# Work handed across three stage borders in a fused perceiver kernel: the wide stage's start, the cell's first weights, the context stage's turned contexts

## The reference

```
x = x + masked_attention(layernorm(x), ctx_1024, ctx_1024, mask)   # 16 heads of 16; 64 batches, 64 tokens each, 256 keys each
x = x + wide_attention(layernorm(x), context)     # 8 heads of 128; 4096 queries against 1024 keys of 192 features
#   sim = q k^T / sqrt(128); sim = (sim - mean) * 1.5 + mean; softmax; times v; times Wout; + bout
x = x + cell(layernorm(x))          # 6 nodes; q, k, v = ew * (earlier node @ We + be), attention of 8 heads,
#   node = act_w * attention + q; the projections We @ Wq (Wk, Wv) of a node can be multiplied ahead: 18 pairs
x = x + context_attention(layernorm(x), ctx_1024) # softmax(x ctx^T) ctx, 64 batches of 64 tokens against 256 keys
x = x + scan(layernorm(x)); x = x + ffn(layernorm(x))              # untouched
```

## Time and profile before

| | us |
|---|---|
| median of 3 executions | 3042.66 (3039.46 to 3043.7) |
| the profiled execution, own time | 3044.71 |
| its span in the trace | 3043.0 |
| mean granted TensorE clock | 0.978 |
| DVE, ACT, POOL busy | 2179.4 (72%), 2042.5 (67%), 1176.4 (39%) |

### The profile page before, as it was taken

How to read it: one execution, slowest core, us unless ns; L and a number is a source line. 1 busy time by engine, 2 the same in 40 slices (tenths; PEclk the granted TensorE clock), 3 DMA queues, 4 the chain that set the end, 5 groups by cost and what they waited for, 6 DMA issues and landing times. The chain is left out here.

```text
span 3043.0 us, 84864 instructions
## 1 busy us (share of the span) xinstructions
PE 2862.5 (94%) x32198; PEld 2233.0 (73%) x32198; DVE 2179.4 (72%) x5344; ACT 2042.5 (67%) x4144; POOL 1176.4 (39%) x962
## 2 busy tenths in 40 slices
PE   8999999799999999999979999999999998789899
PEld 6888888466666666666667887887888887566798
DVE  7888888676777767767636778777778776668543
ACT  6888888686777777777706776676667676333444
POOL 6777777476565555565601010011010000111210
PEclk9999999999999999999989999999999999899899
DMA  4111111187899898898961012111111110651000
GB/s 148 55 54 60 49 60 36 27 133 136 146 165 150 145 152 149 147 161 146 199 224 52 37 44 71 37 44 54 37 44 50 51 37 26 212 169 50 8 22 28
DMA packets 620990, 275.14 MB, mean 90 GB/s; under 512 B 548971, under 2 KB 593958, under 8 KB 620470
## 3 DMA queue, kind: packets, MB, share of 16 engines
...
## 5 line engine op out<-in xcount | busy, mean ns | idle before, releaser
L1335 POOL TENSOR_TENSOR front_parts<-wide_prob,front_parts 128x1024 f16<-128x1024 f32 x256 | 546.2, 2134 | 354.4 <-ACT front_parts L1556 280.1
L1544 ACT ACTIVATE wide_prob<-wide_score,wide_neg_max,wide_s_up 128x1024 f32<-128x1024 f32 x256 | 307.5, 1201 | 147.8 <-DVE wide_neg_max L1657 140.6
L1654 DVE TENSOR_REDUCE wide_row_max<-wide_score 128x1 f32<-128x1024 f32 x256 | 312.6, 1221 | 131.0 <-PE wide_score L1376 130.7
L1376 PE MATMUL wide_score<-wide_kT,wide_qT 128*128 128x512 f16 x1536 | 377.2, 382 | 6.2 <-ACT wide_prob L1544 4.7
L2012 POOL TENSOR_TENSOR cell_w<-cell_w_stage,cell_w 128x1536 fp32r<-128x1536 f32 x23 | 80.4, 3494 | 642.9 <-ACT cell_w L2280 642.9
L637 POOL TENSOR_TENSOR mask_prob<-mask_prob,mask_inv_sum 128x512 f32<-128x512 f32 x256 | 272.2, 1064 | 107.7 <-DVE mask_inv_sum L1020 105.3
L885 ACT ACTIVATE mask_prob<-mask_prob,mask_row_min 128x256 f32<-128x256 f32 x512 | 255.0, 502 | 47.7 <-DVE mask_row_min L968 47.4
L1556 ACT ACTIVATE front_parts<-wide_prob 128x1024 f16<-128x1024 f32 x256 | 269.8, 1054 | 17.6 <-ACT wide_prob L1544 8.1
L1376 PEld LDWEIGHTS wide_score<-wide_kT,wide_qT 128*128 128x128 f16 x1536 | 145.0, 98 | 154.8 <-ACT wide_prob L1544 6.6
L2474 DVE TENSOR_REDUCE cell_row_max<-cell_score 128x8 f32<-128x512 f32 x192 | 131.2, 683 | 160.2 <-PE cell_score L2110 157.9
L968 DVE CUSTOM_DVE_ANT_0 mask_prob<-mask_score,mask_shut 128x256 f32<-128x256 f32 x512 | 189.1, 416 | 3.7 <-issue 3.7
...
## 6 DMA issues: line engine op xcount, KB each, us to landing
...
front_probT<-front_parts SPq DMA_TRANSPOSE x512, 3.3
...
```

The lines of the kernel that those rows point to most:

```text
L1335: pool.tensor_tensor(parts[:, s % 2, LO, :], prob[:, s % 2, :], parts[:, s % 2, HI, :], ALU.subtract).then_inc(part_lo, 1)
L1376: mm = pe.matmul(score[:, s % 2, half * 512:(half + 1) * 512], qT[:, u_par, a, s * P:(s + 1) * P], kT[:, par, b, half * 512:(half + 1) * 5 ...
L1544: act.activation(prob[:, s % 2, :], score[:, s % 2, :], ACT.Exp, bias=neg_max[:, s % 2:s % 2 + 1], scale=s_up[:, 0:1], accum_out=row_sum[: ...
L1654: dve.tensor_reduce(row_max[:, one], score[:, s % 2, :], AX.X, ALU.max).then_inc(max_found, 1)
```

## The change

**Masked to wide.** The scales, rescales, context halves, first k and v weights' halves and block 0's statistics, rstd and normalise are issued in the masked stage's last unit. The search for the first top goes to the masked stage's prologue, so that units 0, 1 and 30 have one each and unit 31 none. The buffers for it are shared with the masked stage's own (its weights, contexts, masks). In the wide prologue the 24 and 8 filling transposes go, and the last of the four k/v parts comes behind the turn of block 1.

**Wide to cell.** A `CellFront` object holds the eight places for pairs of weights from before the masked stage on (masked probabilities live there in between). In the wide stage's last head SP issues one pair a unit, behind the unit's eight transposing DMAs and ahead of the store. One more set of semaphores is cleared behind a barrier after the cell stage.

**Context.** The host hands the contexts over in two tensors: even units plain, odd units plain and turned side by side (1 MB). An odd unit has no context turns on TensorE and no copies of them on ACT and DVE.

```diff
+        self.cT_home = mem.sb("cT", [P, 2, self.CT, KEYS], F16)
+        self.prob = mem.sb("prob", [P, 2, KEYS])
+        self.w_split_home = mem.sb("w_split", [P, 4 * KEYS], F16)
+        self.cT = self.cT_home[0:self.CP]
+        halves = 8 * self.CT * self.DIM
...
+    def tensor_turn_top(self, pe, bank, ident):
+        pe.wait_ge(self.top_found, 4)
+        pe.transpose(bank[0:4, 0:P], self.top[:, :], ident[:, :]).then_inc(self.top_turned, 1)
+
+    def vector_spread_top(self, dve, bank):
+        dve.wait_ge(self.top_turned, 1)
+        dve.tensor_reduce(self.all_top[:, :], bank[0:4, 0:P], AX.X, ALU.max).then_inc(self.top_spread, 1)
+        dve.wait_ge(self.top_spread, 1)
+        dve.tensor_scalar(self.top_row[:, :], self.all_top[:, :].to_broadcast([4, P]), 1.0, None, ALU.mult).then_inc(self.top_spread, 1)
...
+    def scalar_context_hi(self, act):
+
+        act.wait_ge(self.c_loaded, 16)
+        act.wait_ge(self.scale_step, 2)
+        for c in range(self.CT):
+            act.activation(self.cT[:, 0, c, :], self.c_sb[:, c, :], ACT.Copy, scale=self.down[0:self.CP, self.C_AT]).then_inc(self.c_hi, 1)
+
+    def vector_context_lo(self, dve, c):
+        dve.wait_ge(self.c_hi, c + 1)
+        dve.scalar_tensor_tensor(self.cT[:, 1, c, :], self.c_sb[:, c, :], self.down[0:self.CP, self.C_AT], self.cT[:, 0, c, :],
+                                 ALU.mult, ALU.subtract).then_inc(self.c_lo, 1)
...
+class CellFront:
...
+        self.common = mem.sb("common", [P, self.RAW * 2 * MAT])
...
+        self.raw_places = [self.common[:, rows(x * 2 * MAT, 2 * MAT)] for x in range(self.RAW)]
...
+    def load_pair(self, sp, n):
+
+        sp.dma_start(self.raw_places[n % self.RAW], self.sources[2][n]).then_inc(self.raw_loaded[n % self.RAW], 16)
...
+            if last:
+                front.gpsimd_rstd(pool, 0, const)
...
             turn_probs(u, 1)
+            if last:
+                pe.wait_ge(v_copied, UNITS * 2)
+                front.tensor_turn_top(pe, spare, ident)
             scores(u, k, 1)
+            if last:
+                front.tensor_share_top(pe, spare, ident)
 
...
+            if last:
+                act.wait_ge(ctx_split, UNITS)
+                front.scalar_context_hi(act)
...
             copy_turned(u, 5)
+            if last:
+                act.wait_ge(front.w_loaded[0], front.W_LOADS)
+                front.scalar_kv_weights_hi(act, 0)
...
+            else:
+                front.scalar_normalise(act, 0, front.xn_front[:, 0])
...
-            if not last:
+            if last:
+                front.vector_spread_top(dve, spare)
+            else:
...
+            if last:
+                front.vector_scales(dve, spare)
...
+            if last:
+                front.vector_rescales(dve, WIDE_SHARP * front.DIM ** -0.5)
+            else:
                 k_lo(u + 1, 1 - k, 0)
             copy_turned(u, 4)
...
+            if last:
+                dve.wait_ge(y_ready, SUB)
+                front.vector_stats(dve, 0)
...
+            if last:
+                front.vector_context_lo(dve, 0)
...
+            else:
+                front.vector_context_lo(dve, 1)
+                front.vector_kv_weights_lo(dve, 2, 0)
+            if isinstance(u, int) and not last:
+                front.find_top(dve, u + 1 if u <= 1 else 3)
 
...
+        front.find_top(dve, 0)
...
-            if h == HEADS - 1 and n >= 2:
-                store(n - 2)
+            if h == HEADS - 1:
+                cell_front.load_pair(sp, n)
+                if n == 0:
+                    cell_front.load_small(sp)
+                if n >= 2:
+                    store(n - 2)
...
-        pe.wait_ge(top_found, 4)
-        pe.transpose(misc_ps[0:4, 0:P], top[:, :], ident[:, :]).then_inc(top_turned, 1)
-        keep_clock(pe, ident, pv_ps, 24)
-        pe.wait_ge(top_spread, 2)
-        pe.transpose(misc_ps[:, P:P + 4], top_row[:, :], ident[0:4, 0:4]).then_inc(top_shared, 1)
         pe.wait_ge(xn_ready, 1)
         for t in range(DH):
             turn_half(0, t, turn_ps[t])
-        keep_clock(pe, ident, pv_ps, 8)
 
         pe.wait_ge(c_lo, CT)
         pe.wait_ge(kv_w_lo, 2)
-        for i in range(KV):
+        for i in range(KV - 1):
             kv(0, i, first_bank(i))
         pe.wait_ge(xn_ready, 2)
         for t in range(DH):
 
             pe.wait_ge(xn_lo, t + 1)
             turn_half(1, t, turn_ps[t])
+        kv(0, KV - 1, first_bank(KV - 1))
 
         pe.wait_ge(xn_lo, FRONT * DH)
         pe.wait_ge(w_lo, 2)
...
-        normalise(0)
-        act.wait_ge(scale_step, 2)
-        for c in range(CT):
-            act.activation(cT[:, HI, c, :], c_sb[:, c, :], ACT.Copy, scale=down[0:CP, C_AT]).then_inc(c_hi, 1)
-        act.wait_ge(w_loaded[0], W_LOADS)
-        kv_weights_hi(0)
         for t in range(DH):
             turned_hi(0, t, turn_ps[t])
+        weights_hi(0, 0)
+        kv_hi_part(0, 0, first_bank(0), 1)
         normalise(1)
-        weights_hi(0, 0)
-        for i in range(KV):
+        for i in range(1, KV - 1):
             kv_hi_part(0, i, first_bank(i), i + 1)
         for t in range(DH):
             turned_hi(1, t, turn_ps[t])
+        kv_hi_part(0, KV - 1, first_bank(KV - 1), KV)
         act.wait_ge(scale_step, 6)
         query_hi(0, 0)
         exp(0, 0, 0)
...
-        dve.memset(qk_up[:, :], 0.0).then_inc(pv_ready, 2)
-        stats_of(0)
-        spread_top()
-        stats_of(1)
-        find_scales()
-        for c in range(CT):
-            context_lo(c)
-        kv_weights_lo(2, 0)
+        dve.memset(neg_max[:, :], 0.0).then_inc(pv_ready, 2)
+        front.vector_stats(dve, 1)
         for t in range(DH):
             turned_lo(0, t, turn_ps[t])
-        find_rescales()
         weights_lo(2, 0)
-        for i in range(KV):
+        for i in range(KV - 1):
             kv_lo_part(0, i, first_bank(i), i + 1)
         for t in range(DH):
             turned_lo(1, t, turn_ps[t])
-        stats_of(FRONT)
+        kv_lo_part(0, KV - 1, first_bank(KV - 1), KV)
         query_lo(0, 0)
+        front.vector_stats(dve, FRONT)
         for s in range(2):
             find_max(s, s)
...
-        load_pair(0)
-        sp.dma_start(be[:, :, :], b_columns).then_inc(w_loaded, 16)
-        sp.dma_start(ew_sb[:, :], ew.rearrange("c t -> (c t)").partition_broadcast(P)).then_inc(w_loaded, 16)
-        sp.dma_start(act_sb[:, :], act_w.partition_broadcast(P)).then_inc(w_loaded, 16)
-        for n in range(1, 5):
-            load_pair(n)
         sp.dma_start(x_ln[:, :, :], block_rows(x_in[0:BLK, :])).then_inc(x_loaded, 16)
-        for n in range(5, RAW):
-            load_pair(n)
         sp.dma_start(g_row[:, :], ln_g.partition_broadcast(P)).then_inc(rows_loaded, 16)
         sp.dma_start(b_row[:, :], ln_b.partition_broadcast(P)).then_inc(rows_loaded, 16)
         for n in range(RAW, PAIRS):
...
+    def ctxT_of(k):
+
+        if even(k):
+            return ctxT_made[:, k // 2 % 2]
+        return ctx_both[:, k // 2, 2 * HALF:].rearrange("p (h c) -> p h c", h=DH)
...
+            at, wide, source = (0, HALF, ctx_even) if even(k) else (HALF, 2 * HALF, ctx_odd)
+            n = u // 2 if isinstance(u, int) else i * (NBUF // 2) + k // 2
+            sp.dma_start(ctx_both[:, k // 2, at:at + wide], source[rows(n, 1)].rearrange("u p c -> p (u c)")).then_inc(ctx_loaded[k], 16)
...
-            for part in range(3):
-
-                bank = turn[(k * 3 + part) % 4]
+            for part in range(3 if even(k) else 1):
...
-            pe.wait_ge(turn_copied, (u + 1) * 2)
-            pe.wait_ge(rest_copied, u + 1)
+            pe.wait_ge(turn_copied, copies_to(u, k))
+            if even(k):
+                pe.wait_ge(rest_copied, u + 2)
+            else:
+                pe.wait_ge(ctx_loaded[k], loaded(u, k))
...
-            dve.wait_ge(turned, u * 3 + 3)
-
-            dve.tensor_copy(ctxT[:, k % 2, 1, :], turn[(k * 3 + 2) % 4][:, :]).then_inc(rest_copied, 1)
+            if even(k):
+                dve.wait_ge(turned, turns_to(u, k, 2))
+
...
+    ctx = a.pop("ctx_1024").reshape(B // 2, 2, CTX // P, P, D).transpose(0, 3, 1, 2, 4).reshape(B // 2, P, -1)
+    a["ctx_even"] = ctx[0::2]
+    a["ctx_odd"] = np.concatenate([ctx[1::2], a["ctx_turned"][1::2].reshape(B // 4, P, -1)], axis=2)
```

331 lines of the change are left out of this document (176 added, 155 removed).

## The result

The changed kernel takes 3021.38 us (median of 4, 3019.17 to 3023.51) against 3042.33 us (median of 4, 3039.46 to 3043.7). The ratio is 0.994, with an interval of 0.9929 to 0.9952: 21 us faster. The forecast was 3018, in a range of 3009 to 3031. The profiled execution of the changed kernel has a span of 3021.8 us, 21.2 less than before.

A forecast was written before the change was run, and what follows sets the result against it. TensorE, busy 94% of a 3043.0 us span, was taken as the bound, so time could come only from idle stretches or needless work. Terms -11.1 - 6.7 + 1.5 - 8.6 = -24.9 gave 3018 us, range 3009 to 3031.

The forecast's parts named there:

- C: Wide stage's last head: early weight loads in SP's queue cost +1.5 us, bounds 0 and +6.
- D: Context stage: odd units without context turns make short steps 2.83 us against 3.39; -8.6 us, bounds 0 and -15.5.
- units of 14 us or more: Last head: the prediction would be wrong at this unit length; it expected 13.14 to 13.4 us.
- A: Wide stage's start: first scores at +11.9 us instead of 23.2, gain 11.3, masked stage +0.2; net -11.1, bounds -7 and -11.5.
- The rival with half clock: Wide prologue runs at half clock, so its gain is 4.5 us less: 3022 us; chance 0.08.
- B: Cell stage's start: early loads save 7.2 us, a semaphore clear costs 0.5; net -6.7, bounds -5.5 and -7.2.
- a load on top of 0.99 gives 1.13, which was free: Last head: a load added to a store unit's DMA share costs nothing; the last two units reach 1.27.
- The rival at 1 to 3 us a unit: Last head: DMA engines bound it, costing 8 to 24 us instead of 1.5: 3024 to 3040 us; chance 0.07.
- The figure of 261 GB/s: Last head: the skill's transposing DMA rate puts a unit's 2 MB at 8.0 us, making the price 0: 3016.3 us.
- the 11.2 of the prediction: Last head: a unit's transposing DMAs take 11.2 us, from measured share 0.85 x 13.14 us.

The follow-up runs named there:

- ACT's queue: Changed kernel with four early pairs issued by ACT in last-head units 0, 5, 6 and 7, the rest at the cell stage's start: 3022.58 us.
- one pair: Changed kernel with only small loads and pair 0 early, behind the last unit's transposing DMAs; pairs 1 to 7 at the cell stage's start: median 3015.41 us.
- pairs in pieces: Changed kernel with each pair's load cut into four DMAs of 32 partitions, one behind each quarter's two transposing DMAs: 3022.39 us.
- late pairs: Changed kernel with all cell loads back at the start of the cell stage: 3017.94 us, ratio to before 0.9928.
- the context part alone: Kernel before with only the context stage's part of the change: 3035.81 us, ratio 0.9983.

## Why the prediction was right, and where it was not

The time fell in the range, 3.4 us above the forecast. That it came so near is luck in part: two terms that were off, C and D, met 4.5 us that were not in the sum, without which it would have been some 3026. By its own sign ("units of 14 us or more") the prediction was wrong in the last head, where four of the five units behind the first load took 14.35 to 14.9.

- **A, the wide start**: predicted 11.3 and +0.2 in the masked stage, measured 11.2 and -0.4 (by the average of all profiles +0.6, within their spread). Each step came as it was worked out from the rows before: first scores at +12.0 for +11.9. The rival with half clock did not decide. By the rows above the 12 matmuls ran in 2.75 us. In three of the twelve profiles with this prologue they did not: the kernel with ACT's queue has the same 12 in 4.45 us (granted clock 0.50, the 1.2 GHz level, from 568 to 572, against 1.00) and the first scores at +13.2, those with one pair and with pairs in pieces 3.64 and 3.66 us and both +12.7.

```profile
567.18 1.94 PE L1550 MATMUL wide_turn<-const_ident,front_prob 128*128 128x128 f32 x8 [1.55 <-PEq L70]
568.91 4.45 PE L1495 MATMUL wide_score<-front_cT,front_w_split 96*128 96x512 f16 x12
...
580.37 2.75 PE L1517 MATMUL wide_score<-wide_kT,wide_qT 128*128 128x512 f16 x12 [1.57 <-DVE wide_qT L1758]
```

  So the slower level comes some of the time and costs 0.7 to 1.2 us, not 4.5: most of what it adds falls into the wait for block 1's normalise. The Trainium skill's rule ("TensorE: Matmul & The Clock Gate", "What's actually happening"), that half clock is the default, shows in these three profiles and not in the other nine, behind the same 1.55 us of idle time; it did not make the removed filling transposes a loss.
- **B, the cell start**: predicted -6.7, measured -7.1 beside before and -6.7 beside late pairs.
- **C, the price in the last head**: this step failed. Predicted +1.5 with bounds 0 and 6; measured 11.8 in the last head against the profile of before and 11.9 against late pairs, which has everything else alike (the table's +8.3 has the longer heads of before in it). Two things in the step were wrong. The load was priced as a store of its size ("a load on top of 0.99 gives 1.13, which was free"); the runs show that a store costs a unit nothing and a load of the same bytes 0.6 to 1.7 us in the changed kernel's units, and the three loads behind these another 5.6 us together. The busy share that the price was worked out from does not foretell it: before, a unit at a share of 1.13 took 13.14 us, and with the change one at 0.95 takes 14.88. And the step looked for the wait at TensorE's read of the turned probabilities, where there is slack. The slack ends sooner, at ACT's copy into the two `front_parts` buffers that the transposing DMAs have to have read. The rival at 1 to 3 us a unit had the price (12 / 8 = 1.5), at a chance of 0.07. The figure of 261 GB/s from the Trainium skill ("DMA: Bandwidth & Descriptors", "Latency and other measured facts"), by which the term was 0, led further off: in the changed kernel a share of 0.72 in a unit of 13.18 us without plain transfers is 9.5 us for the transposes, between the 8.0 of the page and the 11.2 of the prediction, and neither foretold the price. The measured share of such a unit was 0.85 before and is 0.72 with the change, for the same transposes (see the last section).
- **D, the context stage**: the mechanism was right (short steps 2.85 for 2.83, idle time before attend, 0.26 us for 0.5), the size was off. Long steps are 3.44 instead of 3.39 (0.7 us over 15), and four short steps, from scores to scores 3.0 to 4.3 us, are 2.2 us longer together than the others. Of this 1.6 us stand in the two steps in which DVE waits for a store of y (4.30 and 3.02); the other two (3.11 and 3.20) stand at the same steps in the kernel with the context part alone, and what they wait for is open. With 0.5 us won at the first step that is 8.3 - 0.7 - 2.2 + 0.5 = 5.9, for 8.6. The stage's first scores come 0.9 us later after the cell stage, which was not in the sum.
- **Not in the sum**: the cell's six nodes, -4.5, whose cause is open.

What a load has that a store has not, so that the transposing DMAs behind or beside it land in 7 us, is open: packet length, one queue or two, and burst or spread have been taken out as causes. A load from elsewhere than HBM was not tried.
